# Weight maxima and flags over the partitions by TensorE products, and a row loop moved in the instruction stream

## What is computed

```
qkv    = xn @ w_qkv.T + b_qkv                 # (512, 1536), 16 heads of 32
attn   = softmax(q @ k.T / sqrt(32) + causal) @ v
hidden = silu((xn @ gate_w.T) * gate_s) * ((xn @ up_w.T) * up_s)      # 1408 wide, weights -1, 0, 1
out    = x + (attn @ w_out.T + b_out) + (hidden @ down_w.T) * down_s
```

## Time and profile before

| | us |
|---|---|
| median of 3 runs | 2006.07 (2004.94 to 2008.21) |
| the profiled execution | 2009.29 |
| its span, first to last instruction | 2007.5 |
| TensorE busy in the span | 1894.6 |
| VectorE, ScalarE, GpSimd busy | 1343.0, 1296.2, 1360.8 |

### The profile page before, as it was taken

How to read it: one execution, slowest core, us unless ns; L and a number is a source line. 1 busy time by engine, 2 the same in 40 slices (tenths; PEclk the granted TensorE clock), 3 DMA queues, 4 the chain that set the end, 5 groups by cost and what they waited for, 6 DMA issues and landing times.

```text
span 2007.5 us, 48253 instructions
## 1 busy us (share of the span) xinstructions
PE 1894.6 (94%) x15532; PEld 911.3 (45%) x15532; DVE 1343.0 (67%) x3914; ACT 1296.2 (65%) x2315; POOL 1360.8 (68%) x1098
## 2 busy tenths in 40 slices
PE   4767999999999999999999999999999999999995
PEld 1323444444444444444444444444444444444442
DVE  7775675766767676676767667675766767567663
ACT  2765676666667667676766667676666767666662
POOL 1166676676867667686766868677686866768664
PEclk9888999999999999999999999999999999999997
DMA  8135859677685977768596786868778686877845
GB/s 330 28 65 100 164 104 161 130 127 154 112 153 113 152 139 126 148 114 152 113 158 133 123 146 116 145 125 155 136 121 146 112 151 129 150 141 117 148 85 116
DMA packets 840049, 267.89 MB, mean 133 GB/s; under 512 B 812864, under 2 KB 812864, under 8 KB 839232
## 3 DMA queue, kind: packets, MB, share of 16 engines
q1 hardware_dynamic: 839872, 265.15, 71.4%
HBM read 46.94 MB, written 16.78 MB: 32 GB/s over the span
## 4 chain that ended last, share of the span: by engine, by line
PE 60%; POOL 12%; issue 10%; DVE 7%; SPq 6%; DMA 3%; ACT 2%; DVEq 0%; POOLq 0%; ACTq 0%
PE ps L503 60%; POOL phl L1183 5%; SPq L425 4%; POOL region_b L1157 3%; DMA p_t<-phl 3%; POOL memory L1178 2%; DVE p L1089 1%; SPq L489 1%; DVE memory L873 1%; SPq L491 1%; POOL region_a L1162 1%; POOL rstd L1153 1%; POOL o_hl L1188 1%; DVE hidden_tmp L998 1%; DVE hidden_tmp L1004 1%
## 5 line engine op out<-in xcount | busy, mean ns | idle before, releaser
L503 PE MATMUL ps<-x_t,memory 128*128 128x512 f16 x4384 | 1005.9, 382 | 44.2 <-DVE memory L873 27.4
L1183 POOL TENSOR_TENSOR phl<-p,phl 128x1024 f16<-128x1024 f32 x320 | 683.3, 2135 | 428.9 <-ACT phl L812 428.9
L802 ACT ACTIVATE p<-p,nmax 128x384 f32<-128x384 f32 (+3 forms) x1024 | 529.8, 557 | 282.0 <-DVE nmax L1089 264.7
L503 PEld LDWEIGHTS ps<-x_t,memory 128*128 128x128 f16 x4384 | 408.2, 98 | 541.2 <-issue 94.6
L1089 DVE CUSTOM_DVE_ANT_0 p<-ps,causal,cst 128x384 f32<-128x384 f32 (+3 forms) x1024 | 515.2, 546 | 101.9 <-PE ps L503 77.0
L812 ACT CAST phl<-p 128x1024 f16<-128x1024 f32 x320 | 334.0, 1044 | 45.7 <-DMA p_t<-phl 29.8
L503 PE MATMUL ps<-memory 128*128 128x512 f16 x1408 | 323.9, 380 | 5.2 <-POOL memory L1178 4.3
L1178 POOL TENSOR_TENSOR memory<-hidden_tmp,memory 128x512 f16<-128x512 f32 x176 | 204.9, 1164 | 73.8 <-ACT memory L774 58.5
L1097 DVE TENSOR_REDUCE ps<-ps 128x132 f32<-128x264 f32 (+1 forms) x320 | 122.0, 381 | 182.4 <-PE ps L503 182.4
L503 PEld LDWEIGHTS ps<-vv,p_t 128*128 128x128 f16 x5120 | 187.4, 96 | 96.7 <-issue 24.3
L503 PE MATMUL ps<-vv,p_t 128*128 128x68 f16 (+1 forms) x5120 | 193.6, 185 | 16.5 <-DMA p_t<-phl 16.2
(11 more groups left out here) (65 smaller groups left out, 1307.9 us busy)
## 6 DMA issues: line engine op xcount, KB each, us to landing
region_b<-x SPq DMA_DIRECT2D x32, 1024.0 KB, 6.6
out<-region_b SPq DMA_DIRECT2D x64, 256.0 KB, 2.3
p_t<-phl SPq DMA_TRANSPOSE x640, 3.1
memory<-w_qkv SPq DMA_DIRECT2D x3, 1024.0 KB, 8.8
memory<-down SPq DMA_DIRECT2D x1, 2816.0 KB, 21.5
memory<-gate SPq DMA_DIRECT2D x1, 2560.0 KB, 9.5
memory<-up SPq DMA_DIRECT2D x1, 2560.0 KB, 15.3
x_t<-region_a SPq DMA_TRANSPOSE x64, 3.5
```

Of the source, the lines that this page charges most:

```text
L503: return nc.tensor.matmul(o, lhsT=l, rhs=r, start=start, stop=stop, skip_group_check=True)
L802: last = nc.scalar.activation(cols, cols, ACT.Exp, scale=-1.0, bias=nmax[:, s % 2, i:i + 1])
L1183: g.tensor_tensor(phl[:, s % 2, 1, :], p32[:, s % 2, :], phl[:, s % 2, 0, :], ALU.subtract)\
```

## The change

The five GpSimd reductions are gone. For a pair of maxima TensorE multiplies two columns of `amax` with an identity of 4-byte data, which puts each column in one row of a PSUM bank (2 x 128). VectorE takes the largest of each row, makes the power of two, sets both on the diagonal of a 2 x 2 matrix, and a second product with a matrix of ones gives them to all partitions. A flag is the sum over the partitions, by a one-column product, which VectorE copies to `lo_flag`. Three `turn_max`, three `spread` and two `sum_lo` are put at fixed points of TensorE's list: the first pair ahead of the wait for x, the second ahead of item 8 (q2) and behind the second of its three parts, the third in slot 1 of the first row, the flags with the values of slots 2 and 9. Six products whose result is not read (PE_PAD) stand at the head of TensorE's stream. Constants grow from 5 to 9. The sums `t0` to `t7` move on ScalarE from the first row into the preamble, and S0, F0, F1, O0, g and u steps change places on VectorE.

```diff
+PE_PAD = 6
 DVE_FIRST = [
-    "h8 h9 | | j0 | j1", "h10 j2 | | h11 g0 j3 | j4", "j5 u0 F0 | | O0 |", "g1 | u1 | S0 | g2 u2",
-    "| | w0 w1 g3 | u3", "| w2 | y0 | g4 w3 u4 y1", "w4 | | g5 | u5 w5 y2 y3", "| | Y0 g6 | u6 w6", "| w7 | g7 u7 |",
-    "| | g8 e0 u8 |", "| e1 | g9 | u9 e2 F1", "| | B0 g10 |", "u10 | C0 | |", "| | d0 |", "| | d1 |", "| | |",
+    "O0 h8 h9 | | j0 | j1", "h10 j2 | | S0 | j3 g0 h11", "j4 j5 u0 | | g1 F0 |", "| u1 | | g2 u2",
+    "| | w0 w1 g3 | u3", "| w2 | y0 g4 | w3 u4 y1", "w4 | | g5 | u5 w5 y2 y3", "| | Y0 g6 | u6 w6", "| w7 | g7 u7 |",
+    "| | g8 e0 u8 |", "| e1 | g9 | u9 e2", "| | F1 B0 |", "g10 u10 | C0 | |", "| | d0 |", "| | d1 |", "| | |",
 ACT_FIRST = [
-    "t0 h9 t1 h10 h11 | | | t2 t3 |", "g0 | | t4 | t5 t6 t7 |", "| g1 | u0 | |", "| | g2 | | w0 u1 w1",
-    "u2 g3 | w2 | w3 | | g4", "u3 | | w4 | | w5", "g5 u4 | | | g6 u5 | w6 w7", "| | | |", "u6 | g7 | | u7 |",
+    "h9 h10 h11 | | | |", "g0 | | | |", "g1 | | u0 | |", "| | g2 | | w0 u1 w1 g3", "u2 | w2 | | | g4",
+    "u3 w3 | | w4 | | w5", "g5 u4 | | | g6 u5 | w6 w7", "| | | |", "u6 | g7 | | u7 |", "g8 | | | |",
 POOL_FIRST = [
-    "| |", "| |", "S0 u0 | | F0", "u1 | |", "u2 | |", "u3 | |", "u4 | |", "u5 R0 n0 | |", "u6 n1 | |", "u7 | | n2",
-    "u8 | F1 | n3", "u9 | |", "u10 | l0 | l1 l2 l3", "| |", "| |", "| |", "| |", "| |", "| |", "| |",
+    "| |", "| |", "u0 | |", "u1 | |", "u2 | |", "u3 | |", "u4 | |", "u5 R0 n0 | |", "u6 n1 | |", "u7 | | n2",
+    "u8 | | n3", "u9 | |", "u10 | l0 | l1 l2 l3", "| |", "| |", "| |", "| |", "| |", "| |", "| |",
+SUM_LO_CHUNKS = (2, 9)
-NONE_ACT = ("q0 k0 v2 v3 v0 v1 q1 k1 h0 h1 q2 h2 h3 k2 h4 h5 q3 h6 h7 k3 h8").split()
+NONE_ACT = "q0 k0 v2 v3 v0 t0 t1 v1 t2 t3 q1 t4 t5 k1 h0 h1 t6 q2 h2 h3 t7 k2 h4 h5 q3 h6 h7 k3 h8".split()
+FFN_IN_MAX_ITEM = 8
+        turned_max = ps[0:2, 4, 0:P]
+        spread_two = ps[:, 4, P:P + 2]
+        summed_lo = ps[0:1, 4, 510:512]
...
@@ values (TensorE)
                 if s == 0:
                     pe.wait_ge(sem["v_lo"], at(r, "v_lo", TT))
-                if isinstance(r, int) and r == 0 and s == 0:
-                    pe.wait_ge(consts_done, N_CONSTS)
-                elif s:
+                    if isinstance(r, int) and r == 0:
+                        pe.wait_ge(outs_scaled, 3)
+                if s:
                     pe.wait_ge(sem["o_norm"], at(r, "o_norm", s))
...
+                if isinstance(r, int) and r == 0 and s in SUM_LO_CHUNKS:
+                    sum_lo(SUM_LO_CHUNKS.index(s))
...
+            def turn_max(nth):
+                pe.wait_ge((qkv_batch, ffn_in_batch, outs_batch)[nth], (1, 2, 2)[nth])
+                nc.tensor.matmul(turned_max, lhsT=amax[:, 2 * nth:2 * nth + 2], rhs=identity[:, :], start=True,
+                                 stop=True, skip_group_check=True).then_inc(max_turned, 1)
+            def spread(nth):
+                pe.wait_ge(scaling, 4 * nth + 4)
+                nc.tensor.matmul(spread_two, lhsT=ones[0:2, :], rhs=diagonal[:, nth, :], start=True, stop=True,
+                                 skip_group_check=True).then_inc(two_spread, 1)
+            def sum_lo(col):
+                pe.wait_ge((ffn_lo_found, down_lo_found)[col], 1)
+                nc.tensor.matmul(summed_lo[:, col:col + 1], lhsT=lo_max[:, col:col + 1], rhs=ones[:, 0:1], start=True,
+                                 stop=True, skip_group_check=True).then_inc(lo_summed, 1)
+            pe.wait_ge(consts_done, N_CONSTS)
+            for _ in range(PE_PAD):
+                nc.tensor.matmul(turned_max, lhsT=ones[:, 0:2], rhs=identity[:, :], start=True, stop=True,
+                                 skip_group_check=True)
+            turn_max(0)
+            spread(0)
             pe.wait_ge(sem["x_turned"], at(0, "x_turned", 16 * TT))
             for n, (kind, i) in enumerate(ITEMS["none"]):
+                if n == FFN_IN_MAX_ITEM:
+                    turn_max(1)
...
+                    if n == FFN_IN_MAX_ITEM and k == 1:
+                        spread(1)
...
@@ slots of a row (TensorE)
+                    if mode == "first" and s == 1:
+                        turn_max(2)
                     fill(s, 0)
                     fill(s, 1)
+                    if mode == "first" and s == 1:
+                        spread(2)
...
@@ VectorE
+            def power_of_two(nth, done, shift=1.0):
+                cols = slice(2 * nth, 2 * nth + 2)
+                peak, power = top[:, nth:nth + 1], top_two[:, nth:nth + 1]
+                dve.wait_ge(max_turned, nth + 1)
+                v.tensor_reduce(peak, turned_max, AX, ALU.max).then_inc(scaling, 1)
+                dve.wait_ge(scaling, 4 * nth + 1)
+                v.tensor_scalar(peak, peak, 2.0 ** -60, shift, ALU.max, ALU.mult).then_inc(scaling, 1)
+                dve.wait_ge(scaling, 4 * nth + 2)
+                v.tensor_scalar(power.bitcast(I32), peak.bitcast(I32), 0x7F800000, None, ALU.bitwise_and)\
                     .then_inc(scaling, 1)
+                dve.wait_ge(scaling, 4 * nth + 3)
+                v.tensor_scalar(diagonal[:, nth, :], identity[0:2, 0:2], power, None, ALU.mult).then_inc(scaling, 1)
+                dve.wait_ge(two_spread, nth + 1)
+                v.reciprocal(inv[:, cols], spread_two).then_inc(done, 2)
+                v.tensor_copy(two[:, cols], spread_two).then_inc(done, 1)
                 dve.wait_ge(done, 3)
+            def copy_flag(col):
+                dve.wait_ge(lo_summed, col + 1)
+                v.tensor_copy(lo_flag[0:1, col:col + 1], summed_lo[:, col:col + 1]).then_inc(flags_done, 1)
...
@@ attention_out (VectorE)
                     v.tensor_reduce(o_sums(n), o_halves(n), AX, ALU.add).then_inc(sem["o_sum"], 1)
+                    if isinstance(r, int) and r == 0 and s in SUM_LO_CHUNKS:
+                        copy_flag(SUM_LO_CHUNKS.index(s))
...
@@ GpSimd
+            g.memset(ones[:, :], 1.0).then_inc(consts_done, 1)
+            g.memset(identity[:, :], 1.0).then_inc(consts_done, 1)
+            for n, sign in enumerate((1, -1)):
+                pool.wait_ge(consts_done, 7 + n)
+                g.affine_select(out=identity[:, :], in_=identity[:, :], compare_op=ALU.is_ge, fill=0.0, base=0,
+                                pattern=[[-sign, P]], channel_multiplier=sign).then_inc(consts_done, 1)
-            pool.wait_ge(qkv_batch, 1)
-            all_max(slice(0, 2), 1)
-            pool.wait_ge(ffn_in_batch, 2)
-            all_max(slice(2, 4), 2)
...
-                        elif kind == "S":
-                            pool.wait_ge(outs_batch, 2)
-                            all_max(slice(4, 6), 3)
-                        elif kind == "F":
-                            pool.wait_ge(ffn_lo_found if i == 0 else down_lo_found, 1)
-                            all_lo(i)
```

More of the change, by code:

```diff
@@ L12 @@
 AX = mybir.AxisListType.X
-ABSMAX = bass.bass_isa.ReduceOp.absmax
 P = 128
@@ L286, in block_program @@
         group_max = sb("group_max", [P, len(GROUPS)])
-        amax_all = sb("amax_all", [P, 8])
+        identity = sb("identity", [P, P])
+        ones = sb("ones", [P, P])
+        top = sb("top", [2, 3])
+        top_two = sb("top_two", [2, 3])
+        diagonal = sb("diagonal", [2, 3, 2])
         two = sb("two", [P, 8])
@@ L363, in block_program @@
         outs_batch = ctx.enter_context(nc.semaphore("outs_batch"))
-        max_reduced = ctx.enter_context(nc.semaphore("max_reduced"))
+        max_turned = ctx.enter_context(nc.semaphore("max_turned"))
         scaling = ctx.enter_context(nc.semaphore("scaling"))
+        two_spread = ctx.enter_context(nc.semaphore("two_spread"))
+        lo_summed = ctx.enter_context(nc.semaphore("lo_summed"))
         qkv_scaled = ctx.enter_context(nc.semaphore("qkv_scaled"))
@@ L382, in block_program @@
         block = ctx.enter_context(nc.Block())
-        N_CONSTS = 5
+        N_CONSTS = 9
         N_QKV_SCALED = 6
@@ L608, in values @@
                     pe.wait_ge(sem["v_lo"], at(r, "v_lo", TT))
-                if isinstance(r, int) and r == 0 and s == 0:
-                    pe.wait_ge(consts_done, N_CONSTS)
-                elif s:
+                    if isinstance(r, int) and r == 0:
+                        pe.wait_ge(outs_scaled, 3)
+                if s:
                     pe.wait_ge(sem["o_norm"], at(r, "o_norm", s))
-                else:
+                elif not (isinstance(r, int) and r == 0):
                     pe.wait_ge(sem["o_norm"], at(r - 1, "o_norm", NCH))
+                if isinstance(r, int) and r == 0 and s in SUM_LO_CHUNKS:
+                    sum_lo(SUM_LO_CHUNKS.index(s))
                 pe.wait_ge(sem[f"pt{s % 2}"], at(r, f"pt{s % 2}", 32 * (s // 2 + 1)))
@@ L643, in fill @@
                         if mode == "first" and k == 0 and (kind, i) == ("g", UNFLAGGED):
-                            pe.wait_ge(flags_done, 1)
-                            has_lo["gate, up"] = pe.value_load(lo_flag[0:1, 0:1].bitcast(I32))
```

(28 more changed lines are left out.)

17 lines of the change are left out of this document (3 added, 14 removed), and 4 rows, old and new, of the table ACT_FIRST.

## The result

The changed kernel takes 1992.1 us (median of 4 runs, 1988.57 to 1994.28) against 2006.08 for the kernel before beside it: a ratio of 0.9927, 95% interval [0.991, 0.9945]. That is 14 us faster where 36 were forecast, and outside the range. The profiled execution took 1988.57 us, its span is 1986.8.

A forecast was written before the change was run, and what follows sets the result against it. TensorE was taken as the bound, busy 94% of the span, except in the first row, bound by GpSimd waits and VectorE. 2009.29 less 24.5 (first row) and 12.1 (loop) is 1972.7, as a median 1970 us; range 1963 to 1977.

The forecast's parts named there:

- the loop's: Row loop on TensorE: shifting its head by 56 instructions removes the stall behind the 18th product, 12.1 us gone.
- "slower" rival: Row loop: the head's own block has to be fetched, 34 us back, 2015.5 us; chance 0.05.
- The first row's 24.5 us: First row: without the GpSimd holes around its reductions it runs 24.5 us earlier, 2.4, 4.3 and 1.3 of that included.
- Second scaling: Preamble, second pair of maxima: tanh scale at 53.4 us instead of 50.89, splits of gate and up 1.7 us later.
- First score maximum: VectorE's first score maximum: near 70.9 us instead of 67.88, 3.0 us later.
- Second scores: First row, TensorE's scores of unit 1: start near 80 us instead of 76.65, 3.4 us later.
- The split of 125.36: First row, the VectorE split that started at 125.36 us: starts near 112.3, 13 us earlier.
- the rival in which VectorE binds the first row sooner: First row: VectorE or ScalarE binds sooner, half of the 24.5 us left, 1982 us; chance 0.13.
- Bias products: Late first row, TensorE's bias products: start at about 148.4 us instead of 164.92 and take about 2.7 us.
- The holes: First row, GpSimd idle around three reductions, 6.12 us ahead and 7.60 behind: gone, 32.2 us of chain.
- "The place does not matter": Row loop: shifting it gains nothing or only moves the stall, 1982 us; chance 0.17.
- "Two instructions a product": New products are two instructions each, 28 in all, so the loop stall comes sooner, about 2005 us; chance 0.05.

The follow-up runs named there:

- e9: The changed kernel run again unaltered, with its 6 idle products (shift 56): 1991.16 us, ratio 0.9936 to the kernel before.
- e10: The changed kernel with 56 idle products instead of 6 (shift 256): 1986.26 us, ratio 0.9911 to the kernel before.
- e3: The kernel before with 14 idle products added to TensorE's stream ahead of its loop (shift 56): 2011.15 us, ratio 1.0015.
- e4: The kernel before with 35 idle products added ahead of its loop (shift 140): 1997.73 us, ratio 0.9954.
- e2: The changed kernel with 27 idle products instead of 6 (shift 140): 1977.8 us, ratio 0.9853 to the kernel before.
- e8: The changed kernel with both flags made by GpSimd reductions again and PE_PAD 29 instead of 6 (shift 140): 1991.42 us, ratio 0.9938 to the kernel before.
- e12: The kernel before with 42 idle products added ahead of its loop (shift 168): 1988.35 us, ratio 0.9922.
- e7: The changed kernel with 34 idle products instead of 6 (shift 168): 1969.43 us, ratio 0.9825 to the kernel before.
- e11: The changed kernel with 44 idle products instead of 6 (shift 208): 1970.33 us, ratio 0.9828 to the kernel before.

## Why the prediction was wrong

**The step that failed is the loop's: "From three on (42) the head stands past the boundary, and the next one is then a stretch away that takes longer than the 3.9 us: 12.1 us gone".** Its first half held: four instructions a product, 56 in all, and the stall behind the 18th product vanished. Its second half took the boundary behind the head for the only one that counts. Past it, the head itself stood in a block that the branch had to wait for: 0.7 to 0.85 us in nearly every row at a shift of 56, 1.2 at 32, none from 88 on. That is the mechanism of the "slower" rival, at a fifth of its 3.5 us a row. What was held against that rival, a branch of 361 ns, was a row at the old place and could say nothing of the new one. A second cost had no place in the forecast at all: the other blocks of a row move too, and one now falls on the last transpose of x. By timed runs of one chip the place cost e9 - e10 = 4.9 us (on another chip e3 less the kernel before, 3.5) instead of giving 12.1: a miss of 16 to 17. The 12.1 was also misread: 10.3 of it stood in the rows, 0.79 in each and not 0.93, and 1.81 behind the loop's end; that part did go.

**The first row's 24.5 us** were the right mechanism, too large by 5 or 6. At equal places the timed runs give 19.9 (e4 - e2) and 18.1 (before - e10). Two things made it too large. The profiled execution of before has its loop start at 209.2 us, while the three runs of it with idle products start at 206.5 to 206.8; its first two GpSimd holes, 7.60 and 7.73 us behind the reduction (7.52 and 7.66 of it on the chain of the earlier trace rows), were long ones: in those three runs they are 6.74 to 7.35. Whether execution or place made them so stays open. And at the end of the row 2.4 + 4.3 + 1.3 = 8.0 us were counted beyond the bias products, of which 22.8 - 17.4 = 5.4 came: with the holes gone, TensorE waits 2.65 us for p_t at 169.76 instead.

Step by step, from the profiled execution:

- First maxima: 0.7 earlier forecast, 23.29 to 22.54 measured.
- Second scaling: tanh scale done at 53.4 forecast; it starts at 51.72 and takes 0.23, and in e9 it starts at 53.29; the step was right to within what two executions differ by.
- First score maximum: 70.9 forecast, 68.77 measured. Second scores: 80 forecast, 78.2 measured; TensorE waits 4.04 us for the diagonal there. Both move with the second scaling: in e9 all three are 1.6 later.
- The split of 125.36: 112.3 forecast, 111.06 measured. Two of the four splits ahead of it took 2.3 us and not the 1.7 allowed, and it took 2.71 itself. That was given as a sign of being wrong, but the rival in which VectorE binds the first row sooner still did not come: VectorE had 22 us idle in 61 to 121 us to give.
- Bias products: 148.4 forecast, 147.48 measured, 3.46 us for twelve instead of 2.7.
- The holes: the second halves, which the Trainium skill (GPSIMD Engine Reference, Instruction dispatch) does not name, went with the first ones, and e8 brought both back. So the rows priced the hole better than the page's figure alone.

**The rivals.** "The place does not matter" is out: e3, e4 and e12 change nothing else and reach from 0.9922 to 1.0015. "Two instructions a product" is out by the count. The forecast's 1970 us is what the change gives at a good place (e7, e11: 1969 to 1970); the place chosen here is a bad one.

The fastest version found is the change with 34 idle products, 1969.43 us: 0.9825 [0.9808, 0.9841] of before. 44 can't be told from it.

## What to carry to other kernels

Where a loop's body is long and its engine is full, the position of its first instruction is a parameter of its own: any edit ahead of the loop moves it, so compare two versions at the same position (modulo 256 TensorE instructions here), or sweep it, before an edit is credited with the difference. An "issue" gap at one place of every row and a long branch are two faces of it; when a shift moves the one away, work out where the next boundary comes to stand, at the branch and beside the row's transfers. And price a hole from more than one execution: the 7.60 us of the earlier trace rows were 6.74 in e12, for the same reduction.

## What the runs showed of the hardware

- Where a packet on the instruction queue falls on transposes under way, they often stand still: 1.0 to 1.3 us of almost nothing moved at the two places shown, and 4.8 us to landing for x where the median of that trace is 3.4 (4.1 for p_t in e2, where it is 3.1). In all fourteen traces, from 330 to 1830 us, the transposes stand still for 0.8 us or more 297 times with one issued 1.5 us before and landing 1.5 us after; 277 of these overlap with such a packet, against 18 on average when the packets' times are moved by 3 to 9 us. This is read from records that coincide; no run separates it from the place. The standstill costs only where the transposed data is needed soon after: e7 has one of 0.8 us, too, from 393.0 us on, and TensorE does not wait there.
- The head stall follows the fetch. At shifts of 32 and 56 the last packet ahead of the branch starts 0.5 to 1.8 us before it, and the branch ends 1.4 to 1.7 us behind the packet's end, in all rows of four traces. At 88 and 112 the packet starts 2.2 to 3.2 us ahead, elsewhere 5.4 to 8.2, and there is no stall at the head.
- The price of the branch back depends on the place: 356 to 361 ns at shifts of 0, 140, 168, 208 and 256, some 450 at 88 and 112, 1256 to 1422 at 56 and 1687 at 32. Why the packet comes so late at 32 and 56, and where exactly between 56 and 88 that ends, was not tried.
- Two executions of one kernel differ by 1.6 us in when the second scaling is done (51.72 and 53.29), so a forecast of a step in the first row can't be judged more finely than that.
